# Gated slots on one core: masked products and sums of squares at other places of the step, first state scanned in the step before, statistics first

## What is computed

```python
q, k, v = silu(x @ Wq.T), silu(x @ Wk.T), silu(x @ Wv.T)
f = log_sigmoid(x @ Wf.T) / 8.0
s = 1.0 - exp(f)
S1 = S1 * exp(f)[..., None, :] + k[..., :, None] * s[..., None, :]      # per token
ok = einsum('bhk,bhkm->bhm', q, S1)
qv = softmax(ok, axis=-1)
S2 = S2 * exp(f)[..., :, None] + s[..., :, None] * v[..., None, :]      # per token
ov = einsum('bhm,bhmv->bhv', qv, S2)
o = silu(ov)
out = (o * rsqrt(mean(o * o) + 1e-5) * g_w) @ Wo.T
```

## Time and profile before

| | us |
|---|---|
| median of 3 runs | 4329.46 |
| lowest and highest | 4323.24, 4329.81 |
| the profiled execution | 4343.58 |
| its span in the trace | 4341.9 |
| the layer in that span | 3216.3 to 3674.2 |
| mean granted clock of TensorE | 0.911 |

### The profile page before, as it was taken

How to read it: one execution, slowest core, us unless ns; L and a number is a source line. 1 busy time by engine, 2 the same in 40 slices (tenths; PEclk the granted TensorE clock), 3 DMA queues, 4 the chain that set the end, 5 groups by cost and what they waited for, 6 DMA issues and landing times. The chain is left out here.

```text
span 4341.9 us, 89574 instructions
## 1 busy us (share of the span) xinstructions
PE 3676.8 (85%) x31167; PEld 2202.5 (51%) x31167; DVE 2777.1 (64%) x6198; ACT 2242.0 (52%) x5440; POOL 1946.3 (45%) x1935
## 2 busy tenths in 40 slices
PE   6999999955959999999999999985957775976758
PEld 2333333334935555555555555554845664665436
DVE  6888888854546666666666666655456664655465
ACT  2667666742425555555555555543335552764357
POOL 2222222136436656665665666547431211645165
PEclk9999999965979999999999999985979997887879
DMA  4333433212641111111111111111542222110000
GB/s 96 57 59 60 61 58 57 43 45 75 201 117 43 44 43 40 45 45 40 42 44 44 40 44 45 40 52 58 194 124 67 68 63 47 40 41 5 1 1 40
DMA packets 418240, 252.25 MB, mean 58 GB/s; under 512 B 251187, under 2 KB 344355, under 8 KB 416643
## 3 DMA queue, kind: packets, MB, share of 16 engines
q1 hardware_dynamic: 409156, 228.56, 22.6%
q0 software_dynamic: 8640, 17.97, 1.3%
HBM read 75.12 MB, written 41.75 MB: 27 GB/s over the span
## 5 line engine op out<-in xcount | busy, mean ns | idle before, releaser
L2483 POOL TENSOR_TENSOR ra_prob<-ra_prob,ra_inverse 128x256 f32<-128x256 f32 (+3 forms) x512 | 639.9, 1254 | 637.0 <-DVE ra_inverse L2677 479.1
L2639 ACT ACTIVATE ra_prob<-ra_ps_s,ra_low 128x128 f32<-128x128 f32 (+3 forms) x1024 | 533.1, 529 | 741.8 <-DVE ra_low L2651 741.7
L2299 DVE TENSOR_REDUCE ca_mx<-ca_ps_s 128x2 f32<-128x1024 f32 x512 | 600.4, 1210 | 110.8 <-PE ca_ps_s L2160 110.5
L2225 ACT ACTIVATE ca_pT<-ca_ps_p 128x512 f32<-128x512 f32 x1024 | 547.7, 601 | 220.6 <-PE ca_ps_p L2170 218.7
L2651 DVE TENSOR_REDUCE ra_low<-ra_ps_s 128x2 f32<-128x256 f32 (+3 forms) x512 | 408.1, 818 | 310.8 <-PE ra_ps_s L2565 309.7
L2160 PE MATMUL ca_ps_s<-ca_kst,ca_qst 128*128 128x512 bf16 x1024 | 394.2, 391 | 38.1 <-DVE ca_mx L2299 22.5
L2507 PE MATMUL ra_ps_t<-ident,ra_prob 128*128 128x128 f32 x2560 | 364.2, 281 | 44.1 <-ACT ra_probT L2617 36.2
L2170 PE MATMUL ca_ps_p<-ca_qst,ca_kst 128*128 128x512 bf16 x1024 | 386.2, 382 | 4.0 <-ACT ca_pT L2225 3.9
L2507 PEld LDWEIGHTS ra_ps_t<-ident,ra_prob 128*128 128x128 f32 x2560 | 273.4, 141 | 213.4 <-ACT ra_probT L2617 83.4
L2565 PE MATMUL ra_ps_s<-ra_kz,ra_qz 64*128 64x128 f32 (+3 forms) x2048 | 381.0, 470 | 0.0
L2579 PE MATMUL ra_ps_o<-ra_probT,ra_v 128*64 128x512 f32 (+3 forms) x2048 | 331.7, 445 | 0.0
(11 more groups left out here) (411 smaller groups left out, 7230.7 us busy)
## 6 DMA issues: line engine op xcount, KB each, us to landing
moe_w_own<-moe_w1T SPq DMA_DIRECT2D x142, 256.0 KB
ra_qz<-ra_rot SPq DMA_DIRECT2D x512, 64.0 KB, 2.0
ra_kz<-ra_rot SPq DMA_DIRECT2D x512, 64.0 KB, 2.0
ca_kst<-ca_bounce SPq DMA_DIRECT2D x256, 64.0 KB
ca_bounce<-ca_thirds SPq DMA_DIRECT2D x192, 64.0 KB, 2.9
ca_qst<-ca_bounce SPq DMA_DIRECT2D x64, 192.0 KB
moe_hs<-moe_rows SPq DMA_DIRECT2D x142, 66.0 KB
moe_raw<-in_L_ffn_W SPq DMA_DIRECT2D x32, 256.0 KB, 3.0
```

Of the source, the lines that this page charges most:

```text
L2225: nc.scalar.activation(pT[:, (NS * hp + u) % PRING, :], ps_p[n % NP][:], ACT.Exp).then_inc(sg["drained"], 1)
L2299: nc.vector.tensor_reduce(mx[:, hm % 2, 2 * j:2 * j + 2], ps_s[m % 2][:].rearrange("p (b k) -> p b k", b=2), AX.X, ALU.max)\
L2483: nc.gpsimd.tensor_tensor(at, at, inverse[:, n % PROB, 2 * tile:2 * tile + 2].unsqueeze(2).broadcast_to([P, 2, keys]), ALU.mult)\
L2639: nc.scalar.activation(prob[:, score % PROB, t, head, 0:keys], part(score, t)[:, head, :], ACT.Exp, bias=low[:, score % PROB, at:at + 1], ...
```

## The change

Five things move, and no operation is added or taken away.

- PE: `inside` on `ps_o2` was the last group of a step. It is now in the next step, behind `before` on `ps_o1`, and `before` on `ps_o2` follows behind the turn of `okT`. The sums of squares and the output product stand behind the scores of the first pass; the sums of squares go to the bank `ps_q`, for which `v` now waits for `ovar`. The turn of `qv` stands ahead of the sums with `vx`.
- DVE: the first state's scan and transpose were at a step's beginning for `i3`; they are at the end of the step before, ahead of `f` and `gs`. `ovar` stands behind `ok` and ahead of `sT`.
- ACT: `kn` stands ahead of `oT`, so `oT` is followed by the exponentials.
- POOL: `rs` stands ahead of `osq`.
- The start: the statistics of the first sequence come first on DVE, then the copies of the weights; the buffers are cleared at the end of the first step (`kx`, `vx`) and of the second (`q2m`, `am2x`), and on POOL behind the first `rs`. SP waits for the cleared buffers one by one.

The core of the diff:

```diff
@@ sync @@
-                sp.wait_ge(zeroed, 4)
+                sp.wait_ge(zeroed_pool, 1)
...
                 def body(i0, i1, i2, i3, i4):
+                    if i2 == 0:
+                        sp.wait_ge(zeroed_pool, 2)
+                        sp.wait_ge(zeroed_dve, 2)
+                    if i3 == 0:
+                        sp.wait_ge(zeroed_dve, 4)
@@ tensor @@
                 def body(i0, i1, i2, i3, i4):
-                    if live(i4):
-                        need(pe, "state2_done", i4)
-                        before(ps_o2, lambda n: s2[:, :, n - 1], q2m, "o2_in")
                     if live(i3):
                         need(pe, "s1T_done", i3)
                         before(ps_o1, lambda n: s1T[:, n - 1, :], qm[:, i3 % 3], "o1_in")
                     if live(i4):
-                        need(pe, "osq_done", i4)
-                        need(pe, "kn_ready", i1)
-                        need(pe, "bn_ready", i3)
-                        for c in range(TC):
-                            last = nc.tensor.matmul(ps_t[:, c:c + 1], osq[:, c * P:(c + 1) * P], core.ones[:, 0:1], start=True, stop=True)
-                        last.then_inc(sg["ss_in"], 1)
+                        need(pe, "am2x_landed", i4, EXPAND)
+                        need(pe, "vn_ready", i4)
+                        need(pe, "o_done", i4 - 1)
+                        inside(ps_o2, vn[:, i4 % 3], am2x)
                     if live(i3):
                         need(pe, "ok_done", i3)
-                        need(pe, "ovar_done", i4)
...
                         turn(ps_t, lambda c: okT[:, c * P:(c + 1) * P], "ok_turned")
                     if live(i4):
...
+                        need(pe, "state2_done", i4)
+                        before(ps_o2, lambda n: s2[:, :, n - 1], q2m, "o2_in")
...
+                    if live(i4):
+                        need(pe, "osq_done", i4)
+                        need(pe, "qn_ready", i1)
+                        need(pe, "vn_ready", i2)
+                        for c in range(TC):
+                            last = nc.tensor.matmul(ps_q[:, c:c + 1], osq[:, c * P:(c + 1) * P], core.ones[:, 0:1], start=True, stop=True)
+                        last.then_inc(sg["ss_in"], 1)
...
                     if live(i3):
+                        need(pe, "qv_done", i3)
+                        turn(ps_t, lambda c: qv[:, c * P:(c + 1) * P], "qv_turned")
                         need(pe, "vx_landed", i3, EXPAND)
                         need(pe, "state1_done", i3)
                         sums(vx[:, i3 % 2], "sumv_in")
-                        need(pe, "qv_done", i3)
-                        turn(ps_t, lambda c: qv[:, c * P:(c + 1) * P], "qv_turned")
                     if live(i1):
                         need(pe, "qn_ready", i1)
+                        need(pe, "ovar_done", i4)
...
-                    if live(i3):
-                        need(pe, "am2x_landed", i3, EXPAND)
-                        need(pe, "vn_ready", i3)
-                        need(pe, "o_done", i4)
-                        inside(ps_o2, vn[:, i3 % 3], am2x)
@@ scalar @@
+                    if live(i1):
+                        need(act, "k_turned", i1)
+                        need(act, "kx_landed", i3, EXPAND)
+                        nc.scalar.copy(kn[:, i1 % 2].rearrange("p c d -> p (c d)"), ps_t[:]).then_inc(sg["kn_ready"], 1)
                     if live(i4):
                         need(act, "o2_in", i4)
                         need(act, "y_in", i4 - 1)
                         need(act, "osq_done", i4 - 1)
                         nc.scalar.activation(oT[:], ps_o2[:], ACT.Silu).then_inc(sg["o_done"], 1)
@@ vector @@
-                nc.vector.memset(kx[:], 0.0)
-                nc.vector.memset(vx[:], 0.0).then_inc(zeroed, 1)
-                nc.vector.memset(q2m[:], 0.0)
-                nc.vector.memset(am2x[:], 0.0).then_inc(zeroed, 1)
...
                 def body(i0, i1, i2, i3, i4):
-                    if live(i3):
-                        decay = flat(carry[:, i3 % 2])
-                        need(dve, "sumk_in", i3)
-                        need(dve, "carry_done", i3)
-                        need(dve, "s1T_done", i4)
-                        nc.vector.tensor_tensor_scan(flat(s1[:]), flat(ps_r[:]), decay, 0.0, ALU.add, ALU.mult).then_inc(sg["state1_done"], 1)
...
+                    if live(i4):
+                        need(dve, "ss_in", i4)
+                        need(dve, "ors_done", i4 - 1)
+                        nc.vector.tensor_scalar(ovar[:], ps_q[:, 0:TC], 1.0 / D, EPS, ALU.mult, ALU.add).then_inc(sg["ovar_done"], 1)
...
+                    if live(i2):
+                        need(dve, "sumk_in", i2)
+                        need(dve, "carry_done", i2)
+                        need(dve, "s1T_done", i3)
+                        nc.vector.tensor_tensor_scan(flat(s1[:]), flat(ps_r[:]), flat(carry[:, i2 % 2]), 0.0, ALU.add, ALU.mult).then_inc(sg["state1_done"], 1)
...
+                    if i0 == 0:
+                        nc.vector.memset(kx[:], 0.0).then_inc(zeroed_dve, 1)
+                        nc.vector.memset(vx[:], 0.0).then_inc(zeroed_dve, 1)
+                    if i1 == 0:
+                        nc.vector.memset(q2m[:], 0.0).then_inc(zeroed_dve, 1)
+                        nc.vector.memset(am2x[:], 0.0).then_inc(zeroed_dve, 1)
```

61 lines of the change are left out of this document (27 added, 34 removed).

## The result

The changed kernel takes 4343.34 us (median of 6 runs, 4339.88 to 4346.59). The kernel before, run beside it on the same chip, takes 4325.95 (6 runs, 4313.76 to 4329.81). The ratio is 1.0041, with a 95% interval of 1.0030 to 1.0051: slower by 0.4%, some 17 us, where 4328 was forecast and the range ended at 4341. The profiled run took 4342.79 us.

The account below looks back on a forecast made before the run. The prediction took a loop through several engines, no single full one, as the bound. Full steps +9, start -5.5 and end -5 us sum to -1.5 from the median of 4329.46: 4328 us, range 4315 to 4341.

Parts of the forecast that it names:

- rival (b): Slower: PE idles twice a step and each wait brings a slow stretch; step 27.1, 4342 us; chance 0.16.
- Part 1: Masked products on PE leave the loop: the whole wait for `am2x`, 1.5 us a step, is covered.
- Part 2: DVE's chain up to the turn of `okT`: that turn starts at 15.1 us instead of 18.5, 3.4 gained.
- Part 3: From `okT`'s turn through `ps_o2`, `oT` and exponentials to `qv`'s turn: all 3.4 us given back, step 24.3.
- Part 4: Disturbances in a full step: 0.8 us for stalls and 0.8 for slow clock, making the step 25.9.
- The stall: PE's wait for "issue" among the small matmuls: half of it stays on the path, 0.8 us a step.
- The slow clock: Slow PE stretches over `ps_o2` or `z`, scores and sums of squares: 0.8 us a step, ends 0.3 and 1.8.
- Part 5: Moved sums, turns and queues inside a step, including the turn of `qv` ahead of the `vx` sums: cost nothing.
- +0.7 a step: Net growth of a full pipeline step, to 25.9 us; +9 us over the twelve full steps.
- Part 6: Layer start: first `xn` 6.0 us earlier, 0.5 charged for the moved clears, net -5.5 us.
- Part 7: Layer end, after the sixteenth sequence: parts of DVE's chain fall out, -5 us, ends -8 and -2.

Follow-up runs that it names:

- e2: Changed kernel with POOL's `carry` waiting until DVE has made `bT`; ratio 1.0014 to the kernel before.
- e4: Changed kernel with `carry` behind `bT` and three unused 512-column products on PE ahead of the turn of `qv`; ratio 0.9979 to the kernel before.
- e13: Changed kernel with `carry` on POOL waiting for `q2T`, and `ors` moved ahead of it; ratio 0.9978 to the kernel before.
- e6: Changed kernel with the 120 products into `ps_o2` put ahead of the turn of `okT` again; ratio 0.9981 to the kernel before.
- e10: Kernel before with only the turn of `qv` moved ahead of the `vx` sums; ratio 0.9963 to the kernel before.
- e3: Changed kernel with three unused 512-column products on PE ahead of the turn of `qv`; ratio 1.0005 to the kernel before.
- e1_start: Kernel before with only the new start (statistics first, buffers cleared inside the first steps); 4323.2 us against 4328.23, ratio 0.9983.
- e12: Kernel before, order kept, with two unused 512-column products on PE behind the turn of `qv`; ratio 0.9975 to the kernel before.
- e9_turn_back: Changed kernel with one edit undone, the turn of `qv` behind the `vx` sums again; ratio 1.0031 to the kernel before.

## Why the prediction was wrong, point by point

**The path of the forecast held; two terms on it and a base were wrong.** The order of events is the one forecast, but the outcome is that of rival (b), the slower one with 0.16: PE idles twice a step, 2.4 and 3.6 us where (b) had 2.6 and 3, and a slow stretch follows the longer wait, not the shorter. Its step of 27.1 and its time of 4342 are what was measured (27.10, 4343), but by luck and not by its own sum: that had 0.8 of stall and 1.0 on `ps_o2` in it, and neither came; the way to the second scores lost 1.7 instead of 1.0, and `carry` took the rest.

- **Part 1**, right. No wait for `am2x`; `s1T` ends 11.6 us behind the turn and `ps_o1` starts 0.7 later, behind the turn of `kT`, some 0.6 later than priced beyond the late scores; the wait for `okT` covers it.
- **Part 2**, right. From scores to `okT` 8.88 us (9.0 priced), and the same 8.9 in nearly every variant of after. The turn of `okT` would be at 14.9 with scores on time (15.1 priced); it is at 16.6 because they start 1.7 later. The gain up to that turn, apart from the scores, is 3.56 (3.4 priced).
- **Part 3**, right in all terms but one. Turn to `oT` 2.77 (2.65), `oT` to `eqT` 3.08 (3.07). The term that failed is "From `sT` to `qv` 2.06": it is 3.09, because `eqT` now releases `carry` on POOL in the same instant as `sT` and `bT` on DVE. I took the duration from a step in which `carry` ran while DVE was elsewhere, and asked of the new order only who waits for whom, not who runs beside whom. The trace of before held the warning: the first `bT`, at 3256.9, the only one that met `carry`, took 1.85 us. e2, e4 and e13 show the cause. The Trainium skill (SBUF — State Buffer, Who interferes with whom) states that a DVE instruction with two SBUF inputs contends with a GpSimd instruction that reads SBUF, and its section "SBUF: two separate sides" calls the shared port pair "an exclusive lock": the loser waits it out. The trace agrees in the main: `bT` begins 0.41 us behind `carry` and ends at 3469.72, 0.54 behind `carry`'s end at 3469.18, a little under its own length of 0.69. It also shows that `carry` isn't left alone: it takes 1.66 us in this step, where it took 1.42 in the steps of before. The meeting should have been weighed in the prediction.
- **Part 4**, wrong in both sizes, with errors of opposite sign. The stall, taken at 0.8, is 0: each piece of small products now has a wait or a turn before it (e6, which puts 272 in one piece, brings it back at 1.3). The slow clock, taken at 0.8 with an upper end of 1.8, costs 1.7 at the scores. Sum 1.7 against 1.6: the total of this part came out right by accident. (By itself the clock was just inside its stated ends of 0.3 and 1.8.)
- **Part 5** holds the sentence that failed for the clock: the second scores' wait of 1.15 "covers it just; in a slow stretch it is 0.5 to 1 dearer, inside the ends above". The slow stretch is not an exception: `v` is slow in all twelve steps, the sums in ten. In the step shown it takes turn (+0.45), sums (+0.9) and `v` (+1.0) together, and of the 1.15 of cover the sums in their new place use 1.1 even at full speed, so that nearly all of the slowing reaches the scores. e10 shows that the same edit gains 1.1 us a step in the kernel before, where PE waits 0 to 1.8 us ahead of the turn, e3 that filling the wait brings the scores back to 5.44.
- **The base.** "+0.7 a step" set 25.9 against 25.17, the mean over fifteen intervals. Over the twelve full steps, the ones it was multiplied with, before takes 24.82 in this trace. That alone is 12 x 0.35 = 4.2 us. It is no firmer than one trace: e1_start, with the same full steps, takes 25.17.
- **Part 6**, right: the first `xn` 8.6 us behind the layer's first DMA (14.5 before: the earlier trace rows and 3216.3), 5.9 gained with 6.0 priced, and 4.7 of it left at the first `q2T` (5.5 priced). The first statistics on DVE and the first `xn` on ACT:

```profile
3200.30 0.87 DVE L1849 BATCH_NORM_STATS2 gsa_parts<-X 128x6 f32<-128x128 f32 x4 [1.53 <-PEq L72]
```

```profile
3208.83 1.65 ACT L1768 ACTIVATE gsa_xn<-X,gsa_shift,gsa_rs 128x128 f32<-128x128 f32 x4 [35.69 <-DVE gsa_shift L1869]
```

- **Part 7**, right: the three intervals that aren't full steps lose 4.7 us and the stretch behind the last `q2T` 0.9, 5.7 in all (5 priced).

The sum by the measured terms: 12 x (27.10 - 24.82) = +27.3, start -4.7, end -5.7: +16.9. Predicted were +9, -5.5, -5. (The forecast of 4328 stood on a median of 4329.46. Beside the change the kernel before took 4325.95, so the time itself is 15 us above the forecast and the difference 18.) The 18 us of error, +16.9 against -1.5, are 12 x 1.03 = 12.4 for the meeting of `carry` and `bT`, 4.2 for the base, and small terms. With the first alone added the forecast would have been 4340, inside the range; with both, 4344. These shares are read along the path of one trace. Taken out by an edit, the meeting is worth more (1.84 a step in e13), because the wait ahead of the turn shrinks with it, and the clock's 1.7, which this sum hides behind the stall that didn't come, is worth 1.35 (e3).

**What stays open.** Which engine the 16 KB packets belong to the trace doesn't say; that they come at fixed places of PE's stream is suggested by e12, where two more products on PE moved them, and isn't shown otherwise. The order of the full steps is the same in before and in e1_start; what makes them 24.82 and 25.17 is not shown. It is also open why about the same wait is followed by slow products once and by fast ones another time: in e9_turn_back `v` takes 1.92 us in one step behind a wait of 2.52 and 1.06 in another behind 2.67. In after, behind waits of 3.6, nearly all were slow.

## What to carry to other kernels

When a change lets two engines start from the same signal, look up whether they disturb each other; durations from the old trace hold only for the old neighbours. A wait moved to another place is not free on TensorE: price the instructions behind it at both clock levels, and see which of them stand on the path. Compare steps over the same steps that the sum is multiplied with, and price a DMA trip by its mean over all steps, not by a clean one.

## What the runs showed of the hardware

- DVE products of two SBUF tensors are held up by a POOL product that reads SBUF: `bT` goes from 0.69 to 1.79 us (after), `qv` from 0.69 to 1.22 (e2). So is `sT`, a DVE operation with one tensor and constants: 0.43 us alone, 1.13 to 1.46 in the four steps of after in which `carry` and not `sT` came first.
- Packets of instructions take part in the DMA traffic: 16 KB, 0.9 to 1.6 us long, and in the 19 late steps, where one falls on the four 64 KB transfers of `q2m`, the scores start 0.8 to 1.9 us later. The Trainium skill (Runtime: NRT & Kernel Launch, Instruction fetch mechanics) gives the 16 KB blocks and calls the cost of crossing one "mostly hidden". What these steps show is another cost, on the data that waits for the same DMA engines: 0.55 us of a 24.8 us step.
- More work made the kernel faster twice: 2.7 us of unused products in a wait of 3.6 us (e3), and 1.7 us of them behind the turn (e12).
- 272 small products of TensorE in one piece lost 1.3 us a step to "issue"; 120 + 32 and 120 with a wait between them lost none (after).
